# Down product of the routed experts cut into 128 and 48 rows, the 48 loaded per tile at two partition offsets

## The reference

```python
gu = jnp.einsum('th,eih->tei', x2, w1)            # w1: 16 experts, 2*176 rows of 256
g, u = (gu[..., :I], gu[..., I:])                 # I = 176
act = jax.nn.silu(g) * u
down = jnp.einsum('tei,ehi->teh', act, w2)        # w2: 16 experts, 256 x 176
routed = jnp.einsum('te,teh->th', wfull, down)    # 4 experts of 16 for each token
```

## Time and profile before

| what | us |
|---|---|
| median of three runs | 1269.1 |
| profiled execution, its own time | 1271.58 |
| its span | 1269.8 |
| mean granted TensorE clock | 0.985 of full |

### The profile page before, as it was taken

How to read it: one execution, slowest core, us unless ns; L and a number is a source line. 1 busy time by engine, 2 the same in 40 slices (tenths; PEclk the granted TensorE clock), 3 DMA queues, 4 the chain that set the end, 5 groups by cost and what they waited for, 6 DMA issues and landing times.

```text
span 1269.8 us, 24366 instructions
## 1 busy us (share of the span) xinstructions
PE 1200.0 (94%) x7612; PEld 1005.0 (79%) x7612; DVE 860.2 (68%) x2630; ACT 793.9 (63%) x1971; POOL 578.1 (46%) x845
## 2 busy tenths in 40 slices
PE   6899998989999999999999999999998889999987
PEld 5745454568989999999998999989997768999962
DVE  5666877737667766787666886677875955555535
ACT  3466777657766777677776777776776534444422
POOL 3052645444334535346542447342463356666650
PEclk9889999989999999999999999999999989999998
DMA  4477777631552011112211112111123236777766
GB/s 150 138 223 231 229 231 223 197 104 64 169 162 67 34 68 34 67 35 101 68 65 37 61 57 91 62 48 53 34 89 99 70 118 119 118 118 118 118 106 221
DMA packets 111682, 139.54 MB, mean 110 GB/s; under 512 B 11269, under 2 KB 94725, under 8 KB 111429
## 3 DMA queue, kind: packets, MB, share of 16 engines
q1 hardware_dynamic: 97108, 119.10, 30.3%
q0 software_dynamic: 14448, 18.88, 9.2%
HBM read 63.36 MB, written 61.87 MB: 99 GB/s over the span
## 4 chain that ended last, share of the span: by engine, by line
PE 67%; DVE 9%; ACT 7%; POOL 6%; DMA 4%; issue 4%; SPq 3%; POOLq 0%; ACTq 0%; DVEq 0%
PE bank L1441 45%; PE bank L1523 5%; PE bank L1827 4%; PE bank L1645 4%; PE bank L1490 3%; DMA raw_qkv<-in_qkvo 2%; DVE bank L1086 2%; POOL sum_rows L721 2%; ACT p L926 1%; PE bank L1510 1%; ACT pT L811 1%; PE bank L1517 1%; POOL xs_rows L659 1%; DVE hs L1299 1%; POOL w_hl L513 1%
## 5 line engine op out<-in xcount | busy, mean ns | idle before, releaser
L1086 DVE CUSTOM_DVE_ANT_0 bank<-bank,mask 128x512 f32<-128x512 f32 (+3 forms) x512 | 235.6, 522 | 49.5 <-PE bank L1510 36.3
L917 ACT ACTIVATE p<-bank,stat 128x512 f32<-128x512 f32 (+3 forms) x256 | 131.5, 526 | 132.3 <-DVE stat L1086 132.3
L512 POOL CAST w_hl<-raw_qkv 128x512 fp32r<-128x512 f32 x96 | 58.7, 611 | 316.0 <-DMA raw_qkv<-in_qkvo 173.1
L1441 PE MATMUL bank<-xT,w_hl 128*128 128x512 f32 x768 | 189.4, 395 | 2.4 <-POOL w_hl L513 2.4
L1441 PEld LDWEIGHTS bank<-xT,w_hl 128*128 128x128 f32 x768 | 144.1, 188 | 36.7 <-POOL w_hl L513 2.8
L721 POOL DMA_INDIRECT sum_rows<-mid,goal x79 | 122.8, 1555 | 70.9 <-DVE mid L1405 68.9
L1441 PE MATMUL bank<-pT,v 128*128 128x128 f32 (+3 forms) x768 | 137.1, 327 | 0.0
L926 ACT ACTIVATE p<-p,stat 128x512 f32<-128x512 f32 (+3 forms) x256 | 123.1, 553 | 14.7 <-DVE stat L1302 14.7
L1441 PE MATMUL bank<-qk 128*128 128x512 f32 (+3 forms) x768 | 129.4, 317 | 2.6 <-DVE pT L1286 2.6
L1441 PEld LDWEIGHTS bank<-qk 128*128 128x128 f32 x768 | 119.2, 189 | 11.3 <-DVE v L1280 2.8
L513 POOL TENSOR_TENSOR w_hl<-raw_qkv,w_hl 128x512 fp32r<-128x512 f32 x96 | 124.1, 1293 | 7.8
(11 more groups left out here) (232 smaller groups left out, 2455.4 us busy)
## 6 DMA issues: line engine op xcount, KB each, us to landing
xs_rows<-blank SPq DMA_DIRECT2D x31, 1040.0 KB, 5.0
raw_qkv<-in_qkvo SPq DMA_DIRECT2D x32, 768.0 KB, 5.3
xrow<-xs_rows SPq DMA_DIRECT2D x79, 130.0 KB, 2.5
raw_o<-in_qkvo SPq DMA_DIRECT2D x32, 256.0 KB, 3.3
sum_rows<-blank SPq DMA_DIRECT2D x3, 2176.0 KB, 9.8
stk<-xT SPq DMA_DIRECT2D x96, 64.0 KB
stk<-k_hl SPq DMA_DIRECT2D x96, 64.0 KB
yl<-sum_rows SPq DMA_DIRECT2D x24, 256.0 KB, 6.2
```

Of the source, the lines that this page charges most:

```text
L512: link(pool.tensor_copy(hi, raw))
L917: act.activation(p2[:, n % 2, POFF[qi]:POFF[qi + 1]], s2(t), ACT.Exp, scale=-1.0, bias=stat2[:, 0, n % 2, t:t + 1], accum_out=stat2[:, 1, ...
L1086: return dve.tensor_tensor_reduce(scores, scores, mask[:, TB - scores.shape[1]:], scale=-1.0, scalar=-2.0 * MASKED, op0=ALU.add, op1=ALU.m ...
L1441: ins = pe.matmul(out, a, b, start=start and i == 0, stop=stop and i == len(pairs) - 1, **kw)
```

## The change

The 176 rows are now cut as 128 and 48. For the 128, `w2r` holds 128 rows for each expert. For the 48 (REST), a DRAM buffer `w2x_rows` gets RX = 112 rows for each expert: rows 0 to 47 are the rest rows for output columns 0 to 127, rows 64 to 111 the same rest rows for output columns 128 to 255, and zeros between. `load_tile` fetches the block of the tile's expert with a second DMA. The turned activation has the 48 rows at partitions 0 to 47 and again at 64 to 111 (DVE writes them twice, `sl` is 240 wide). `down` is then four matmuls of 128 columns: two over 128 rows, into bank 6 (first half of the columns) and bank 7 (second half), and two over 48 rows, one at partitions 0 to 47 into bank 6, one at 64 to 111 into bank 7. As each tile now uses both banks, `down(i)` waits for y of tile i - 1, and y is written by two instructions. The last quarter of w2 is loaded before the first tile. The rows of `w2x_rows` are gathered from DRAM to DRAM during the second attention.

```diff
+            def gather_rest(e):
+                for half in range(2):
+                    for g, k, p, done, m in down_pieces(e, P, REST):
+                        row, col = e * RX + 64 * half + done, 2 * C * P + P * half
+                        sp.dma_start(w2x_d[row:row + m, :], moe_d[g, p:p + m, k, col:col + P]).then_inc(w2x_in, 16)
             for j in range(1, N2 // 2):
+                if 8 <= j < 8 + E // 2:
+                    gather_rest(2 * j - 16)
+                    gather_rest(2 * j - 15)
...
             def load_w2(q):
-                sp.wait_ge(f_u, SHR * (q + 1))
-                if q == B - 1:
-                    sp.wait_ge(r_lg, B)
+                sp.wait_ge(f_u, SHR * (q // 2 + 1))
...
                 sp.dma_start(xt[:, i % NX, :], xs_d[ds(row, P), :]).then_inc(e_x[i % NX], 16)
+                sp.dma_start(w2x[:, i % NX, :], w2x_d[ds((row >> CAP_BITS) * RX, RX), :]).then_inc(e_x[i % NX], 16)
-            for q in range(B - 1):
+            for q in range(B):
                 load_w2(q)
...
-            for i in range(NX // 2):
-                load_tile(i)
-            load_w2(B - 1)
-            for i in range(NX // 2, NT):
+            for i in range(NT):
                 load_tile(i)
...
-                    dve.tensor_tensor(sl[:, i % 2, :], sl[:, i % 2, :], bank[i % 2][:, EI:2 * EI], ALU.mult)\
+                    link(dve.tensor_tensor(sl[:, i % 2, P + 64:], sl[:, i % 2, P:EI], bank[i % 2][:, EI + P:2 * EI],
+                                           ALU.mult))
+                    dve.tensor_tensor(sl[:, i % 2, 0:EI], sl[:, i % 2, 0:EI], bank[i % 2][:, EI:2 * EI], ALU.mult)\
                        .then_inc(e_h, 1)
...
-                    dve.tensor_scalar(yt[:, m % NY, :], bank[6 + m % 2][:, 0:D], xt[:, m % NX, D + 1:D + 2], None,
-                                      ALU.mult).then_inc(e_y, 1)
+                    for half in range(2):
+                        cols = slice(P * half, P * (half + 1))
+                        ins = dve.tensor_scalar(yt[:, m % NY, cols], bank[6 + half][:, cols], xt[:, m % NX, D + 1:D + 2],
+                                                None, ALU.mult)
+                    ins.then_inc(e_y, 1)
...
-                if i >= 2:
-                    pe.wait_ge(e_y, i - 1)
-                for h in range(2):
-                    ins = pe.matmul(bank[6 + i % 2][:, 0:D], ht[:, i % 2, P * h:P * (h + 1)],
-                                    w2r[:, ds(expert[i], 1), h, :].rearrange("p a n -> p (a n)"),
-                                    start=h == 0, stop=h == 1)
+                if i >= 1:
+                    pe.wait_ge(e_y, i)
+                for half in range(2):
+                    cols = slice(P * half, P * (half + 1))
+                    pe.matmul(bank[6 + half][:, cols], ht[:, i % 2, 0:P],
+                              w2r[:, ds(expert[i], 1), cols].rearrange("p a n -> p (a n)"), start=True, stop=False)
+                for half in range(2):
+                    rows, cols = slice(64 * half, 64 * half + REST), slice(P * half, P * (half + 1))
+                    ins = pe.matmul(bank[6 + half][:, cols], ht[rows, i % 2, P:2 * P], w2x[rows, i % NX, :],
+                                    start=False, stop=True)
                 ins.then_inc(e_dn, 1)
```

More of the change, by code:

```diff
@@ L55, in sandwich_kernel @@
     NSUM = 3
-    H2E = EI // 2
+    REST = EI - P
+    RX = 64 + REST
     NSTK = 4
@@ L331, in routed_pieces, with down_pieces @@
                     k += m
-        def down_pieces(e):
-            for h in range(2):
[L336 to L342, removed]
+        def down_pieces(e, first, n):
+            done = 0
+            while done < n:
+                row = SHI + e * EI + first + done
+                k, p = row // P, row % P
+                m = min(P - p, n - done)
+                yield k // MGC, k % MGC, p, done, m
+                done += m
         @block.sync
@@ L376, in _ @@
             sp.wait_ge(d_blank, 2)
+            sp.wait_ge(d_blank, 2)
+            sp.dma_start(w2x_d.rearrange("(e r) n -> e r n", r=RX)[:, REST:64, :],
+                         blank[0:E + 1, 0:P].unsqueeze(1).to_broadcast([E + 1, 64 - REST, P])).then_inc(d_zero, 16)
+            for row, m in ((0, REST), (64, REST)):
+                sp.dma_start(w2x_d[E * RX + row:E * RX + row + m, :], blank[0:m, 0:P]).then_inc(d_zero, 16)
             sp.wait_ge(stk_zero, 3)
@@ L424, in load_tile @@
                 sp.dma_start(xt[:, i % NX, :], xs_d[ds(row, P), :]).then_inc(e_x[i % NX], 16)
-            for q in range(B - 1):
+                sp.dma_start(w2x[:, i % NX, :], w2x_d[ds((row >> CAP_BITS) * RX, RX), :]).then_inc(e_x[i % NX], 16)
+            for q in range(B):
                 load_w2(q)
+            sp.wait_ge(f_u, SHR * (B - 1))
+            sp.wait_ge(w2x_in, 16 * sum(2 * len(list(down_pieces(e, P, REST))) for e in range(E)))
             sp.wait_ge(r_tabi, 1)
@@ L1421, in _ @@
                 tiles = slice(TPB * b, TPB * (b + 1))
+                stats = []
                 for half in range(2):
                     dve.wait_ge(t_sum, 2 * b + half + 1)
-                    for j in range(2):
-                        ins = dve.bn_stats(st6[:, TPB * b + 2 * half + j, :], sums(b, half)[:, D * j:D * (j + 1)])
-                        ins.then_inc(t_st, 1)
-                dve.wait_ge(t_st, TPB * (b + 1))
+                    stats += [dve.bn_stats(st6[:, TPB * b + 2 * half + j, :], sums(b, half)[:, D * j:D * (j + 1)])
+                              for j in range(2)]
+                link(*stats)
                 ask_root(tiles)
@@ L1835, in turn_h @@
                     pe.wait_ge(e_htc, i - 1)
-                for h in range(2):
-                    ins = pe.transpose(bank[4 + i % 2][0:H2E, P * h:P * (h + 1)], sl[:, i % 2, H2E * h:H2E * (h + 1)],
-                                       ident[:, :])
+                for h, m in ((0, P), (1, RX)):
+                    ins = pe.transpose(bank[4 + i % 2][0:m, P * h:P * (h + 1)], sl[:, i % 2, P * h:P * h + m], ident[:, :])
                 ins.then_inc(e_ht, 1)
```

28 lines of the change are left out of this document (15 added, 13 removed).

## The result

| | before | after |
|---|---|---|
| median of 4 runs, us | 1268.58 (1265.78 to 1270.26) | 1282.45 (1280.64 to 1283.26) |
| profiled execution, us (its span) | 1271.58 (1269.8) | 1280.64 (1278.9) |
| granted clock over the span | 0.985 | 0.986 |

The change makes the kernel slower: ratio 1.011, with a 95% interval of 1.0088 to 1.0131, that is 11 to 17 us of 1268.6. The forecast was 1281.0, with a range of 1273 to 1290.

The account below looks back on a forecast made before the run. TensorE's queue was taken to bound the routed stage, `down` counting 1:1. Tiles +12.2, end +0.5 and start -0.7 made +12.0 us: 1283.6 against the profiled execution, 1281 us as median, range 1273 to 1290.

Parts of the forecast that it names:

- The four 128-row passes, 0.45: In `down`: the two 128-row matmuls run as four passes of 128 columns at 0.11 us each, 0.45 together.
- The switch in, 0.20: In `down`, from 128-row to 48-row matmuls: 0.09 us lost plus 0.11 of exposed weight load, per tile.
- The pairs, 0.22: In `down`: the four passes of the two 48-row matmuls run side by side, costing two slots, 0.22 us.
- The switch out, 0.15: From the 48-row matmuls to the transposes behind `down`: 0.09 us lost plus 0.06 of exposed load, per tile.
- The sum over the tiles: Routed stage: 76 of the 79 tiles at +0.16 us each, +12.2 us, bounds +5.3 and +16.
- The end, +0.5: Last three tiles: the last added product and split y lie uncovered on the path, +0.5 us.
- rival C: Routed stage: VectorE's chain or the DMA engines take over, +3 to +8 us on top, 1287 us; chance 0.04.
- The start, -0.7: Stage start: earlier w2 load removes a 1.7 us gap, second DMAs delay first tiles; net -0.7 us, bounds -1.7 and +1.
- The long scatter: Before the first tile load: one 3.72 us scatter of sorted rows might shorten, up to 2.7 us; none counted.
- A: Routed stage: the shape switch is hidden or does not happen, period 2.08 to 2.16 us, 1257.5 us; chance 0.07.
- A2: In `down`: switch costs only 0.09 us each way, loads hidden, period unchanged, 1269 us; chance 0.06 including mixtures near no change.
- rival B: In `down`: 48-row passes do not pair as assumed, one slot more, +8.4 us, 1289 us, without overlap 1298; chance 0.11.

## Why the prediction was right

- *What bounds the stage.* PE's queue, and `down` counts 1:1. Borne out: every edit of PE's passes moved the period by what the passes moved (2.30, 2.42, 2.60, 2.64 us), and a wait that was taken away moved nothing.
- *The four 128-row passes, 0.45.* They start 0.108, 0.110 and 0.112 apart: 0.44 for four. The 0.11 read from products of 32 columns carried over.
- *The switch in, 0.20.* The first pair starts 0.205 after the last 128-row pass (0.09 lost), and takes 0.373 where the second takes 0.272: 0.10 of load in the open. *The pairs, 0.22:* the matmuls of a pair start 7 ns apart, the second pair 0.213 behind the first, in which the open load is contained. *The switch out, 0.15:* 0.203 to the turn of h, whose first transpose takes 0.332 instead of 0.272, so 0.06 for the load that I had bounded by 0 and 0.11. The period came to 2.420 where 2.43 was forecast: unrounded, 0.958 us until the turn of h and 0.054 for its longer first step make 1.01, against 0.863 before, so +0.149.
- *The sum over the tiles.* 74 intervals of +0.147 are +10.9 us, where I had 76 x 0.16 = +12.2; the last three intervals are +0.16, +0.20 and +0.20, +0.56 together. With the start of the stage (below) this makes the last `down` 11.1 us later in the profiled pair.
- *The end, +0.5.* Besides those +0.56, y of the last tile ends 1.91 us after the last `down` starts, where it was 1.72: +0.19. So the end cost 0.75, and the last y comes 11.3 us later, where the sum had +12.0.
- *VectorE, 0.* y ends 0.67 us before the next `down`; forecast 0.69. Busy time per tile is 113.91 / 71.5 = 1.6 us, less than the 1.8 I had, because neighbouring instructions overlap. The kernel with its wait two tiles back shows that the cover was enough.
- *SP and DMA, 0.* 0.80 x 2.42 = 1.94 us of DMA time per tile, under the 2.1 allowed. The kernel in one shape asks for the same in 2.30 us and keeps its rhythm, so rival C had no ground.
- *The start, -0.7.* The gap at the fifth tile went (first `down` to second from 4.03 to 2.42: -1.6) and the first `down` is 1.3 later (1049.23 after 1047.96): -0.3. The direction and the parts held, the delay of the first tiles was under-estimated: tile 0 was turned no later than before (1040.38 after 1040.44), but tile 1, which waits for its second DMA, 0.7 later (1042.34 after 1041.62), and the clock, which falls to half in the wait, came back later too. The windows from 1042 on, after the change:

```profile
1042.00:1046.00 4.00, 3.58 (x12) 3.12 (x13) 0.81 (x4) 1.01 (x3) 0.00 (x0) 0.50 0.39 95
1046.00:1050.00 4.00, 4.00 (x23) 3.81 (x22) 1.71 (x6) 1.49 (x5) 0.00 (x0) 0.69 0.49 120
```

and before:

```profile
1042.00:1046.00 4.00, 3.90 (x15) 3.53 (x14) 1.19 (x4) 1.09 (x3) 0.00 (x0) 0.50 0.53 155
1046.00:1050.00 4.00, 3.21 (x19) 2.67 (x17) 1.65 (x5) 1.58 (x5) 0.14 (x1) 0.92 0.37 110
```

Both run at 0.50 of the clock (1.2 GHz) after PE has waited for the first rows; in the second window the granted clock is 0.69 in the mean after the change and 0.92 before. The forecast had no term for this.
- *The long scatter.* It takes 3.90 us after the change, so nothing came back of it, and to count none was right:

```profile
1030.14 3.90 POOL L674 DMA_INDIRECT xs_rows<-xrow,idx  x1 [0.30 <-issue]
```

- *The gathers, 0.* In all 768 such products of the second attention PE waits 3.3 us for split weights, once (before 2.4). The 13 us of slack held.

```profile
L1462 PE MATMUL bank<-xT,w_hl 128*128 128x512 f32 x768 | 189.4, 395 | 3.3 <-POOL w_hl L528 3.3
```

- *Rivals.* A and A2 fall with the kernel that only changes shape, which pays +0.325 a tile with nothing else in it. B falls with the unpaired one: two slots more. C falls as said.

What I had wrong in the cycle of the earlier trace rows: the four transposes hold PE for 0.36 us until `up` starts, and `up` for 1.05, where I had 0.43 and 0.97. The sum is the same and no term used them.

What I had wrong in the list of signs: PE was to show 0.2 us of idle per tile. It shows none, 173.00 of 173, because the ends of the passes are modelled and reach over the gap. The loads' rows (PEld) show it.

The profiled pair differs by 9.1 us and the medians by 13.9. The routed stage accounts for 11.1 (last `down` to last `down`); what follows the last `down` took 43.9 us before and 41.9 after in these two executions, and 41.6 to 48.3 in the other kernels, whose edits leave the last sum and the normalisation as they are. The difference between 11 and 14 us is inside the interval and has no cause that these traces show. So the mechanism and its terms held, by the traces; that the median came within 1.5 us of 1281 is in part luck.

The Trainium skill, TensorEngine Tiling (Array Packing), section Key Properties, says that a change of the tiling mode drains TensorE. The traces agree and give it a size for matmuls of this kind: 0.09 us each way and 0.04 to 0.10 for the load behind it. The Trainium skill, TensorE: Matmul & The Clock Gate, section The mechanism, says that packed matmuls start and end in program order. Starts 7 ns apart are in order, and yet both passes of a float32 pair overlap. My step from that order to rival B was the wrong one: with both matmuls over the same rows, passes start 0.11 apart, so two that start 7 ns apart belong to different matmuls: the first passes of both run side by side, then the second passes. Rival B would have added 8 us by my estimate.

## What to carry to other kernels

A matmul over a part of TensorE's rows was not cheaper by its rows: a trip into the 64-row shape and back cost 0.33 us in this kernel, as much as three passes of 128 columns. Two pairs did not earn that back, nor did four pairs in a trip (1275 us against 1269 before); running the same product in the full shape was better than one trip per tile (1273 us against 1282), with timing alone shown, as that kernel's sums are not the reference's. Before grouping work to save such a trip, look at what the shortest step then leaves for the sequencer: a register load and a wait that hid behind matmuls cost 0.36 us in every short step, and showed only as "issue" on the weight loads. And take a change apart: its issue order at the start, which was a side matter, was the only edit of this study that came out faster than the kernel before.

## What the runs showed of the hardware

- Which matmuls lost time beside 128-row ones went by their rows: 112 and 128 rows follow each other 0.111 us apart for 128 columns, and passes of 256 columns over 88 rows are followed by a 128-row one after the same 0.215 as by each other; next to 48 and 64 rows 0.09 is lost.
- The loss at a change is the same into and out of the small shape, 0.09 us, whether the passes are 128 or 256 columns wide. The load in the open costs 0.10 us for float32 weights on the way in, 0.06 for the transposes' on the way out in the kernel after and 0.04 in the one that only changes shape.
- Reading a number into a register of TensorE took its sequencer 0.6 us from the load to the check of the bounds, and 0.85 us to the first weight load that uses it. With two tiles together the first weight load of `up` behind it waited 0.36 us in each short step, with nothing else named that it waited for.
- With two tiles together PE's own rows in the routed window were busy for 168.6 of 173 us, where the kernels paced by PE show 171.9 or more: a stall of the sequencer of 0.36 us leaves only 0.1 to 0.3 of idle in these rows, and the loads' rows are the ones to read.
